# The layer norm ahead of the deep stage, moved into that stage and split into five parts

## The reference, cut to what matters

```python
x = L0_attn_x                                            # 16 sequences, 256 tokens, 128 columns
x = layernorm(x + L0_attn(x))
x = layernorm(x + L0_ffn(x))                             # experts
x = layernorm(x + L1_attn(x))                            # feature maps; this norm is moved
x = layernorm(x + deep(x))

def deep(x):                                             # 6 layers
    for i in range(6):
        x = attn_layer(shift_tokens(x), ...) + x         # q, k, v projections, l2norm, rotary, window of 32
        x = ffn_layer(shift_tokens(x), ...) + x
    return x
```

## Time and profile before

| | us |
|---|---|
| median of 3 runs | 4784.36 |
| lowest and highest | 4775.87, 4785.08 |
| the profiled execution | 4782.15 |
| its span | 4780.4 |
| busy in the span: PE, DVE, ACT, POOL | 4240.7, 4081.5, 3053.0, 3026.4 |

### The profile page before, as it was taken

The page is one execution under the profiler, slowest core; times in us unless marked ns, Lnnn a source line. Parts: engine busy times, 40 slices in busy tenths (PEclk is TensorE's granted clock), DMA queues, the critical chain, the costliest instruction groups (busy, mean ns, idle before and its releaser), DMA issues.

```text
span 4780.4 us, 164817 instructions
## 1 busy us (share of the span) xinstructions
PE 4240.7 (89%) x70208; PEld 3352.6 (70%) x70208; DVE 4081.5 (85%) x6282; ACT 3053.0 (64%) x5515; POOL 3026.4 (63%) x1586
## 2 busy tenths in 40 slices
PE   5698699999668999999999999999989999999996
PEld 4565377877656777777777777777767777777775
DVE  4344699999789998999999999899999999999995
ACT  3365333333156777777777777777777777777773
POOL 0222566666267777677777777767677677777762
PEclk9699799999889999999999999999999999999998
DMA  1234000000023233332333323332242332423232
GB/s 50 78 127 141 0 1 0 0 0 0 19 61 70 61 74 88 72 74 62 75 86 74 75 64 90 74 77 66 65 100 62 75 69 65 96 67 78 64 67 66
DMA packets 237661, 302.78 MB, mean 63 GB/s; under 512 B 92500, under 2 KB 127832, under 8 KB 236504
## 3 DMA queue, kind: packets, MB, share of 16 engines
q1 hardware_dynamic: 221752, 247.08, 22.6%
q0 software_dynamic: 15264, 46.14, 3.1%
HBM read 50.37 MB, written 28.84 MB: 17 GB/s over the span
## 4 chain that ended last, share of the span: by engine, by line
DVE 41%; PE 15%; issue 8%; POOL 5%; ACT 3%; DMA 0%; POOLq 0%; DVEq 0%; SPq 0%
DVE raw L1906 10%; DVE raw L1913 8%; DVE mx L1964 3%; DVE ss L1900 3%; DVE E L1970 3%; PE shared L1565 3%; PE acc L1672 2%; DVE den L1977 2%; POOL spare L2129 2%; PE sco L1640 2%; POOL raw L2137 2%; DVE hT L2027 2%; PE shared L1567 2%; PE shared L1566 2%; ACT raw L1783 1%
## 5 line engine op out<-in xcount | busy, mean ns | idle before, releaser
L2137 POOL TENSOR_TENSOR raw<-raw,rs 128x1024 f32<-128x1024 f32 x384 | 793.4, 2067 | 885.5 <-DVE rs L1934 549.3
L2129 POOL TENSOR_TENSOR spare<-raw,table 128x1024 f32<-128x1024 f32 x384 | 971.9, 2541 | 62.8 <-DVE raw L1913 47.1
L1913 DVE TENSOR_TENSOR raw<-raw,spare 128x1024 f32<-128x1024 f32 x384 | 736.5, 1918 | 13.2
L1906 DVE TENSOR_TENSOR raw<-raw,table 128x1024 f32<-128x1024 f32 x384 | 668.2, 1740 | 89.3 <-POOL spare L2129 87.6
L1783 ACT ACTIVATE raw<-shared 128x512 f32<-128x512 f32 x768 | 463.4, 603 | 297.7 <-PE shared L1567 268.4
L1565 PE MATMUL shared<-wqkv_lo,xT_hi 128*128 128x512 f32 x1152 | 550.2, 478 | 57.6 <-DVE xT_lo L1943 48.1
L2154 POOL TENSOR_TENSOR E<-E,rden 128x512 f32<-128x512 f32 x384 | 553.7, 1462 | 30.6 <-DVE rden L1979 30.5
L1900 DVE TENSOR_REDUCE ss<-spare 128x16 f32<-128x1024 f32 x384 | 463.6, 1207 | 46.9 <-ACT spare L1788 46.4
L1620 PE MATMUL trn<-ident,raw 128*128 128x128 f32 x3072 | 484.4, 280 | 7.6 <-POOL raw L2137 4.0
L1566 PE MATMUL shared<-wqkv_hi,xT_lo 128*128 128x512 f32 x1152 | 462.9, 402 | 0.1
L1788 ACT ACTIVATE spare<-shared 128x512 f32<-128x512 f32 x768 | 461.5, 601 | 1.9 <-DVE ss L1900 1.9
(11 more groups left out here) (208 smaller groups left out, 9734.1 us busy)
## 6 DMA issues: line engine op xcount, KB each, us to landing
Vw<-V SPq DMA_DIRECT2D x1344, 128.0 KB
xs<-X SPq DMA_DIRECT2D x144, 128.0 KB, 2.1
Vw<-V SPq DMA_DIRECT2D x192, 64.0 KB
e_plain<-in_L_ffn_W SPq DMA_DIRECT2D x16, 704.0 KB, 4.7
split_hi<-e_high POOLq DMA_DIRECT2D x16, 704.0 KB, 5.9
split_lo<-e_low POOLq DMA_DIRECT2D x16, 704.0 KB, 7.1
wqkv_hi<-split_hi POOLq DMA_DIRECT2D x30, 256.0 KB, 3.1
wqkv_lo<-split_lo POOLq DMA_DIRECT2D x30, 256.0 KB, 3.2
```

The source lines that it names most:

```text
L1906: dve.tensor_tensor(x, x, table[:, part, 0, k][:, None, :].to_broadcast([P, H, HD]), ALU.mult).then_inc(cos_part, 1)
L1913: dve.tensor_tensor(x, x, t2[:, part], ALU.add).then_inc(summed, 1)
L2129: pool.tensor_tensor(dst, src, by[:, None].to_broadcast([P, H, 2, 32]), ALU.mult).then_inc(sin_part, 1)
L2137: pool.tensor_tensor(x, x, rs[:, at:at + H][:, :, None].to_broadcast([P, H, HD]), ALU.mult).then_inc(rotated, 1)
```

## The change

The call of `norm_stage` ahead of the deep stage goes. In `deep_stage` the same norm is made in five parts, with the tiles of the last norm: blocks 0 to 3 (two sequences) among the fills at the beginning, then 4, 8, 8 and 8 blocks at steps of the first body, statistics at steps 3, 9, 16 and 23 and the normalisation four steps later, with the power on POOL's queue at the step of the statistics. A `bring` waits until the part that holds its sequence is normalised. The copy of X to HBM moves behind the fourth `bring` and waits for all parts; the first addition into X waits for it. The four tables are loaded ahead of the first `bring`.

```diff
@@ -1163,6 +1163,8 @@
 STEPS = 16
+FIRST_PARTS = ((0, 4), (4, 8), (8, 16), (16, 24), (24, 32))
+FIRST_STEPS = (3, 9, 16, 23)
...
+def first_part(n):
+
+    return [lo <= 2 * n < hi for lo, hi in FIRST_PARTS].index(True)
...
+        first_stats = sem("first_stats")
+        first_means = sem("first_means")
+        first_kept = sem("first_kept")
+        first_powered = sem("first_powered")
+        first_normed = sem("first_normed")
...
@@ -1430,7 +1442,6 @@
             sp.dma_start(mask32, c["mask"][:, 0:P]).then_inc(const_in, 16)
-            sp.dma_start(kept, X[:].rearrange("p b d -> p (b d)")).then_inc(x_kept, 16)
...
@@ -1488,11 +1499,16 @@
                 sp.wait_ge(const_in, 16)
+                if q.n + d < NSEQ:
+                    sp.wait_ge(first_normed, count(first_part(q.n + d) + 1))
                 sp.dma_start(xs[:], X[:, bass.ds(2 * q.place(d), 2), :]).then_inc(staged, 16)
 
             def body(q):
                 if q.has(3):
                     bring(q, 3)
+                if q.n == 0:
+                    sp.wait_ge(first_normed, count(len(FIRST_PARTS)))
+                    sp.dma_start(kept, X[:].rearrange("p b d -> p (b d)")).then_inc(x_kept, 16)
...
@@ -1510,10 +1526,10 @@
+            for j in range(4):
+                load_table(0, j)
             bring(Pair(0, 0), 0)
             bring(Pair(0, 0), 1)
-            for j in range(4):
-                load_table(0, j)
             load_wo(0)
...
@@ -1980,6 +1996,8 @@
                 dve.wait_ge(projected, count(q.n + d + 1))
+                if q.n + d == 0:
+                    dve.wait_ge(x_kept, 16)
...
@@ -2032,6 +2050,27 @@
+            def first_statistics(i):
+
+                lo, hi = FIRST_PARTS[i]
+                for b in range(lo, hi):
+                    t = dve.bn_stats(last_st[:, b], X[:, b])
+                t.then_inc(first_stats, 1)
+                dve.wait_ge(first_stats, count(i + 1))
+                for b in range(lo, hi):
+                    t = dve.bn_aggr(last_mv[:, b], last_st[:, b])
+                t.then_inc(first_means, 1)
+                dve.wait_ge(first_means, count(i + 1))
+                dve.tensor_scalar(last_ve[:, lo:hi], last_mv[:, lo:hi, 1], EPS_LN, None, ALU.add).then_inc(first_kept, 1)
+
+            def first_normal(i):
+                lo, hi = FIRST_PARTS[i]
+                dve.wait_ge(first_powered, count(i + 1))
+                for b in range(lo, hi):
+                    t = dve.tensor_scalar(X[:, b], X[:, b], last_mv[:, b, 0:1], last_rstd[:, b:b + 1],
+                                          ALU.subtract, ALU.mult)
+                t.then_inc(first_normed, 1)
...
+            def first_of(q, at):
+                if q.n == -2 and at in FIRST_STEPS:
+                    first_statistics(1 + FIRST_STEPS.index(at))
+                if q.n == -2 and at - 4 in FIRST_STEPS:
+                    first_normal(1 + FIRST_STEPS.index(at - 4))
...
@@ -2089,20 +2134,22 @@
+                    first_of(q, at)
                     last_of(q, at)
 
             dve.memset(half, -0.5).then_inc(filled, 1)
+            first_statistics(0)
             dve.memset(xs4[0:1, :, 64:D], 0.0).then_inc(filled, 1)
...
                 dve.memset(Vw[64 * hp:64 * hp + WIN, :, 0, 0], 0.0).then_inc(filled, 1)
+            first_normal(0)
             dve.wait_ge(const_in, 16)
...
-            dve.wait_ge(x_kept, 16)
             body(Pair(0, -1))
...
@@ -2201,11 +2248,19 @@
+                    if q.n == -2 and at in FIRST_STEPS:
+                        first_powers(1 + FIRST_STEPS.index(at))
...
+            def first_powers(i):
+                lo, hi = FIRST_PARTS[i]
+                pool.wait_ge(first_kept, count(i + 1))
+                pool.tensor_tensor(last_rstd[:, lo:hi], last_ve[:, lo:hi],
+                                   half[:, 0:1].to_broadcast([P, hi - lo]), ALU.pow).then_inc(first_powered, 1)
...
@@ -2214,6 +2269,8 @@
+            pool.wait_ge(filled, count(1))
+            first_powers(0)
             load_w1(0)
...
@@ -2264,7 +2321,6 @@
-        norm_stage(nc, X, "_n2")
```

## The result

| | before | after |
|---|---|---|
| median of 13 runs each, us | 4784.36 | 4771.31 |
| lowest and highest | 4773.81, 4790.94 | 4768.13, 4774.46 |
| the profiled execution | 4782.15 | 4770.35 |
| its span | 4780.4 | 4768.7 |
| from the norm's first statistics to TensorE's first deep transposition | 32.56 | 9.76 |

The ratio of after to before is 0.9978, with a 95% interval from 0.9970 to 0.9986: about 10.5 us faster, between 6.7 and 14.3. It is not the quotient of the two medians in the table, which lie 13.05 us apart. The last four lines are differences of starts in the two profiled executions. They are counted from the first statistics of the moved norm (1283.70 before, 1285.37 after), because the stages ahead of it, which are the same code, took 1.67 us longer in the execution after.

A forecast was written before the change was run, and what follows sets the result against it. VectorE was taken as the bound, with 41% of the chain that ended last against TensorE's 15%. 22.8 us won at the front less 14.0 for the late parts gives 8.8: 4775.6 us from the median 4784.36, range 4767.5 to 4783.0.

The forecast's parts named there:

- the front: Seam from feature to deep stage, up to TensorE's first deep transposition: TensorE starts 22.8 us earlier.
- the late parts: Norm of blocks 4 to 31, made beside the first projections: costs 14.0 us.
- rival 1: First deep projections: normalisations run beside POOL, late parts cost only 8.9, gain 13.9 us, 4770.5; chance 0.30.
- The work without a wait: Ahead of the second low part, VectorE has no idle time for part 2's statistics and normalisation, part 3's statistics: 6.9 us.
- Part 2's power: In POOL's queue beside the first cosine pair: holds up one addition, 1.1 us.
- Part 1's normalisation: On VectorE behind the first low part: waits for POOL's first sine, 0.7 us.
- rival 2: First deep projections: normalisations alternate with POOL one by one, reductions late, late parts 17.4, gain 5.4 us, 4779.0; chance 0.20.
- Part 3's normalisation: Behind the second low part: pushes the scale and sine the next cosine waits for, 1.8 us net.
- Part 4's statistics, power and normalisation: Ahead of the third low part: statistics and power 1.2 us; normalisation pushes the sine between two cosines, 2.3 us.
- a part as a whole: First deep projections: each part's normalisations take turns with POOL as one group; late parts cost 14.0 us.
- Rival 3: At the front: xs shares queues with tables and w1 loads, again takes 6.2 us; gain 4.8, 4779.6; chance 0.05.
- Rival 4: Deep stage: TensorE's later clock is granted lower, 1.2% eats the 8.8 us; at 0.955, 4794 us; chance 0.05.

The follow-up runs named there:

- both together: Changed kernel with part 1 normalised earlier, parts 2 to 4 normalised on ScalarE, and fills and tables at the front reordered: 4760.59 us, ratio 0.9952.

## Why the prediction was right, point by point

The forecast was 8.8 us, from 22.8 won at the front and 14.0 lost to the late parts. The traces give 9.9 at the seam, from 22.8 and 13.0; the times give 10.5, between 6.7 and 14.3. The measured 4771.31 lies within the range and 4.3 below the forecast. It lies only 0.8 above the 4770.5 of rival 1, whose mechanism is wrong: the time alone could not choose between the two, the traces do. Faster by over 0.2% had 0.42 and less than that 0.52; the ratio of 0.9978 lies just beyond that bound, with an interval that takes in both sides.

- **The front**: 22.8 forecast, 22.80 measured. VectorE resumed 2.46 us after its first statistics, 2.5 were worked out. The prediction's terms up to the end of the normalisations come to 1291.1 and not to the 1291.3 that it goes on with; measured and counted the same way it is 1291.2, since aggregation and the addition of epsilon took 0.6 instead of 0.4. xs landed in 2.1. The copy's share of 4 us is shown by the run that moved it alone. VectorE was the bound: its four normalisations ended at 1292.91, xs was issued at 1292.99, and the tables were out at 1292.55, so SyncE stood 0.4 us behind it where 0.7 were worked out.
- **The work without a wait** (part 2's statistics and normalisation, part 3's statistics): 6.9 forecast. In the change 2.43, 1.93 and 2.43 were added there, 6.8.
- **Part 2's power**, 1.1 forecast: nothing. It was POOL's power that waited (2.54 instead of 1.6 us, at 1311.78), while VectorE's addition behind the cosine kept its 1.22.
- **Part 1's normalisation**, 0.7 forecast, 3.0 in rival 2: 2.4. The four operations took turns with the two sines one by one, as rival 2 said; the reductions behind came late by that much.
- **Part 3's normalisation**, 1.8 forecast, 3.0 in rival 2: 1.5, although it too went one by one. The cosine that followed came 11.78 us behind the low part, against 10.32 before.
- **Part 4's statistics, power and normalisation**, 1.2 and 2.3 forecast, 3.5 together: 2.4. The addition of epsilon waited 1.94 us for a sine, which was in no term: I had priced the statistics by rows taken where POOL was at rest. But the cosine behind it, which before had waited for the first sine of a pair and then taken 3.38 us beside the second, now came when both sines were over and took 1.21. Counted to that cosine's start, statistics and power cost 2.15; counted to its end, nothing. The normalisation took 4.20 us, of which 2.40 in its first operation beside a sine, and waited 0.27 for the power; the sum behind it took 1.23 instead of 3.28. Counted from the cosine's end, that is 2.4. Before, then after:

```profile
1356.32 3.38 DVE L1906 TENSOR_TENSOR raw<-raw,table 128x1024 f32<-128x1024 f32 x1 [2.13 <-POOL spare L2129]
...
1362.13 3.28 DVE L1913 TENSOR_TENSOR raw<-raw,spare 128x1024 f32<-128x1024 f32 x1
```

```profile
1347.88 1.21 DVE L1922 TENSOR_TENSOR raw<-raw,table 128x1024 f32<-128x1024 f32 x1
...
1355.98 1.23 DVE L1929 TENSOR_TENSOR raw<-raw,spare 128x1024 f32<-128x1024 f32 x1
```

So the total of the late parts (14.0 against 13.0) was close by luck, because single terms missed on both sides: part 1's was 1.7 too low, part 2's power and part 4 were 1.1 too high each. The way of waiting that the sum was priced by, a part as a whole, was not what happened. The question on which I had made them hang was answered by the trace: a tensor_scalar with scalars from SBUF waits for POOL like the small one of the earlier trace rows. Rival 1 falls with operations of 2.4 us. The rule of the Trainium skill, "SBUF — State Buffer", section "Who interferes with whom", by which the engine that comes second at the shared ports fully blocks until the other's instruction is over, fits: part 3's operations are 0.34 us or as long as the POOL operation beside them (1.95 beside a scale of 1.90, 2.44 beside a sine of 2.40). Rival 2 had the way of waiting right and its price too high by 4.4 us, mainly because it let part 2's power (1.1) and the normalisations of parts 3 (3.0 against 1.5) and 4 count in full. Rival 3 falls with the landing of 2.1 us. Rival 4 falls too: from 2000 to 3000 us the granted clock was 0.99 after and 0.98 before.

What stays open is the difference of some us between seam and time. Against the one profiled execution of before, the shift at the last low part is 12.8 us for the change (9.9 at the seam), 10.8 for the moved copy (4.0) and 26.2 for both together (18.2), but 23.9 for the late parts left out (22.9). It grew in all nine profiled kernels, by 1.1 to 8.8 us; but the scatter of the one execution of before stands in each of these numbers. Steps between low parts differ by about 0.5 us from one execution to the next (32.42 or 32.96, 36.6 or 37.1), and 96 of them make the scatter of the runs. Whether a part of it is more than scatter was not tested.

## What to carry to other kernels

Look for what else stands in the serial stretch before paying to split the work: 7.4 of the 9.9 us came without a split, and 4 of them from one DMA issued ahead of the one that mattered. Work put "beside" other work costs what the engine has no wait for, plus the waits that it takes on itself; a run that leaves the moved work out says how much that is. Where two engines shut one another out, a row of small operations meets each operation of the other in turn, so put them where the other engine rests, or on a third engine: here that, with part 1 moved and the front reordered, took the kernel to 4760.59 (ratio 0.9952) from the change's 4771.31 (0.9978).

## What the runs showed of the hardware that I had not expected

A tensor_scalar of 8 columns (0.17 us alone) took 2.11 and 2.15 us beside a POOL operation, so a small operation is held up by about as much as one of 128 columns (up to 2.44). The reverse happens too: a power of 8 columns on POOL took 1.63 us beside low parts and 2.54 or 2.64 beside VectorE's cosine products. ScalarE's normalisation of 8 blocks took 3.2 us with POOL at work or not.
